# Attention probabilities scaled in place by VectorE before a plain transpose, instead of turned by a matmul with a diagonal

## The reference, cut to what matters

```python
q = apply_rope(split_heads(x @ Wq)); k = apply_rope(split_heads(x @ Wk)); v = split_heads(x @ Wv)
sim = jnp.einsum('bid,bjd->bij', q, k) * scale
sim = jnp.where(causal[None], sim, -jnp.inf)
attn = jax.nn.softmax(sim, axis=-1)
out = jnp.einsum('bij,bjd->bid', attn, v)
```

## Time and profile before

| | us |
|---|---|
| median of three runs | 1790.22 |
| the profiled execution | 1788.28 |
| its span in the trace | 1786.5 |
| PE busy (share) | 1525.2 (85%) |
| DVE busy | 1250.3 (70%) |
| ACT busy | 995.8 (56%) |
| POOL busy | 1019.2 (57%) |

### The profile page before, as it was taken

The page is one execution under the profiler, slowest core; times in us unless marked ns, Lnnn a source line. Parts: engine busy times, 40 slices in busy tenths (PEclk is TensorE's granted clock), DMA queues, the critical chain, the costliest instruction groups (busy, mean ns, idle before and its releaser), DMA issues. The chain is left out here.

```text
span 1786.5 us, 31373 instructions
## 1 busy us (share of the span) xinstructions
PE 1525.2 (85%) x11301; PEld 1440.1 (81%) x11301; DVE 1250.3 (70%) x2526; ACT 995.8 (56%) x2138; POOL 1019.2 (57%) x814
## 2 busy tenths in 40 slices
PE   5389999999999999999499999999998937689129
PEld 4279999999999998998399999999987836688029
DVE  6547676868677877776346766666678569559896
ACT  4547575657575757665355555455544434459552
POOL 4479586969687777864466767766765633000000
PEclk8679999999999999999699999999999968899569
DMA  6490000000001001000465555555554331003313
GB/s 237 147 300 19 18 19 25 31 25 30 25 14 38 13 22 33 4 31 10 154 177 143 144 136 146 135 147 140 140 136 107 71 96 35 18 1 130 104 52 113
DMA packets 86129, 150.44 MB, mean 84 GB/s; under 512 B 7992, under 2 KB 63608, under 8 KB 85720
## 3 DMA queue, kind: packets, MB, share of 16 engines
q1 hardware_dynamic: 75464, 134.62, 24.6%
q0 software_dynamic: 10512, 13.83, 4.6%
HBM read 111.88 MB, written 49.91 MB: 91 GB/s over the span
## 5 line engine op out<-in xcount | busy, mean ns | idle before, releaser
L1534 POOL TENSOR_TENSOR expert_w_low<-expert_raw,expert_w_high 128x768 fp32r<-128x768 f32 x152 | 288.3, 1946 | 170.3 <-ACT expert_w_high L1359 164.3
L835 ACT ACTIVATE expert_raw<-psum,neg_max 120x376 f32<-120x376 f32 (+2 forms) x384 | 176.0, 479 | 99.3 <-DVE neg_max L996 99.2
L664 PE MATMUL psum<-diag,expert_raw 128*128 128x128 f32 (+2 forms) x1536 | 198.9, 279 | 8.2 <-DVE diag L1005 7.3
L1012 DVE TENSOR_TENSOR pt_low<-psum,pt_high 128x752 fp32r<-128x752 f32 x128 | 120.5, 941 | 118.1 <-ACT pt_high L844 118.1
L1506 DVE TENSOR_TENSOR expert_act_low<-expert_act,expert_act_high 128x384 fp32r<-128x384 f32 x152 | 140.1, 921 | 80.0 <-ACT expert_act_high L1397 79.4
L664 PEld LDWEIGHTS psum<-diag,expert_raw 128*128 128x128 f32 (+2 forms) x1536 | 180.3, 190 | 17.9 <-DVE diag L1005 11.2
L1397 ACT ACTIVATE expert_act_high<-expert_act 128x384 fp32r<-128x384 f32 x152 | 79.8, 525 | 204.7 <-DVE expert_act L1501 203.5
L1318 PE MATMUL psum<-slots_high,expert_w_high 128*128 128x384 f32 x608 | 160.1, 344 | 16.6 <-DVE expert_act L1501 15.4
L936 POOL TENSOR_TENSOR qk_low<-rotated,qk_high 128x376 fp32r<-128x376 f32 x128 | 144.1, 1126 | 47.1 <-ACT qk_high L828 44.3
L959 POOL TENSOR_TENSOR rotated<-expert_raw 128x376 f32<-128x376 f32 x128 | 127.9, 1000 | 56.8 <-ACT expert_raw L822 42.6
L1318 PE MATMUL psum<-slots_low,expert_w_high 128*128 128x384 f32 x608 | 156.4, 338 | 0.0
(11 more groups left out here) (296 smaller groups left out, 4422.6 us busy)
## 6 DMA issues: line engine op xcount, KB each, us to landing
expert_raw<-in_experts SPq DMA_DIRECT2D x152, 384.0 KB, 3.1
x_slots<-in_c_slots SPq DMA_DIRECT2D x4, 3168.0 KB, 29.4
slot_rows<-x_slots SPq DMA_DIRECT2D x19, 396.0 KB, 4.6
up_spill<-held SPq DMA_DIRECT2D x5, 1128.0 KB, 5.0
held<-up_spill SPq DMA_DIRECT2D x5, 1128.0 KB, 5.7
attn_x<-tok_xt SPq DMA_DIRECT2D x6, 752.0 KB, 4.0
x_parts<-attn_x SPq DMA_DIRECT2D x6, 752.0 KB, 4.6
patch<-in_patches SPq DMA_DIRECT2D x8, 376.0 KB, 7.0
```

The costliest lines, as they stand in the source:

```text
L664: last = pe.matmul(psum[0:nj, BANK_PT + bank, at:at + ni], probs[0:ni, h % 2, src:src + nj], diag[0:ni, h % 2, it, 0:ni], start=True, stop ...
L835: last = act.activation(probs[0:ni, h % 2, at:at + P * it + ni], score_bank(h % 2, it), ACT.Exp, bias=neg_max[0:ni, h % 2, it:it + 1], acc ...
L1012: dve.tensor_tensor(pt[1][:, h % 2, :, :], psum[:, BANK_PT:BANK_PT + 2, 0:TOK], pt[0][:, h % 2, :, :].bitcast(F32), ALU.subtract).then_inc ...
L1534: pool.tensor_tensor(w[1][:, g % RING, :], raw[:, g % RAW, :], w[0][:, g % RING, :].bitcast(F32), ALU.subtract).then_inc(w_low, 1)
```

## The change

The diagonals go. In their place DVE multiplies each tile of `probs` by the reciprocals of its rows, in place, with a per-row scalar: three `tensor_scalar` operations per head, of 128x128, 128x256 and 120x376. PE's six matmuls per head with the diagonal become six transposes against the constant identity. PE's `turn` waits for the third of the three operations. The `diag` tile (128 x 768 f32) is no longer allocated.

```diff
-        diag = sb("diag", [P, 2, TILES, P])
...
-                    pe.wait_ge(diag_made, 16 * b + h + 1)
+                    pe.wait_ge(probs_scaled, TILES * (16 * b + h + 1))
...
-                            last = pe.matmul(psum[0:nj, BANK_PT + bank, at:at + ni],
-                                             probs[0:ni, h % 2, src:src + nj],
-                                             diag[0:ni, h % 2, it, 0:ni], start=True, stop=True)
+                            last = pe.transpose(psum[0:nj, BANK_PT + bank, at:at + ni],
+                                                probs[0:ni, h % 2, src:src + nj], ident[0:ni, 0:ni])
...
-                def diagonals(b, h):
+                def scale_probs(b, h):
 
                     dve.wait_ge(exp_made, 16 * b + h + 1 + CR_EXP)
                     dve.reciprocal(inv_sum[:, h % 2, 0:TILES], row_sum[:, h % 2, 0:TILES]).then_inc(inv_made, 1)
                     dve.wait_ge(inv_made, 16 * b + h + 1)
-                    dve.tensor_tensor(diag[:, h % 2, :, :],
-                                      ident[:].rearrange("p (o n) -> p o n", o=1).broadcast_to((P, TILES, P)),
-                                      inv_sum[:, h % 2, 0:TILES].rearrange("p (t o) -> p t o", o=1)
-                                      .broadcast_to((P, TILES, P)), ALU.mult).then_inc(diag_made, 1)
+                    for it in range(TILES):
+                        ni, at = TILE_ROWS[it], PROBS_AT[it]
+                        rows_of = probs[0:ni, h % 2, at:at + P * it + ni]
+                        dve.tensor_scalar(rows_of, rows_of, inv_sum[0:ni, h % 2, it:it + 1], None,
+                                          ALU.mult).then_inc(probs_scaled, 1)
```

More of the change, by code:

```diff
@@ L497, in attention @@
          raw_made, swap_made, rope_made, rot_made, qk_high, qk_ready, scores_made, max_made, exp_made,
-         inv_made, diag_made, turned, pt_high, pt_ready, mixed, o_high, o_ready, out_made, out_kept) = (
+         inv_made, probs_scaled, turned, pt_high, pt_ready, mixed, o_high, o_ready, out_made, out_kept) = (
             sem(n) for n in
@@ L501, in attention @@
             "raw_made swap_made rope_made rot_made qk_high qk_ready scores_made max_made exp_made "
-            "inv_made diag_made turned pt_high pt_ready mixed o_high o_ready out_made out_kept".split())
+            "inv_made probs_scaled turned pt_high pt_ready mixed o_high o_ready out_made out_kept".split())
         CR_RAW, CR_ROT, CR_SCORES, CR_EXP, CR_TURN, CR_PT, CR_MIX, CR_O, CR_QK = 1, 2, 4, 1, 2, 1, 2, 1, 2
@@ L1170, in step @@
                     if more or c + 1 < PAIRS:
-                        diagonals(b, 2 * c + 2)
-                        diagonals(b, 2 * c + 3)
+                        scale_probs(b, 2 * c + 2)
+                        scale_probs(b, 2 * c + 3)
                     if projects:
@@ L1183, in _ @@
                 maxima(0, 0)
-                diagonals(0, 0)
-                diagonals(0, 1)
+                scale_probs(0, 0)
+                scale_probs(0, 1)
                 for b in range(BATCH):
```

## The result

The changed kernel takes 1812.76 us (median of four runs, 1812.33 to 1818.67) against 1789.43 us before (four runs). The ratio is 1.0138, 95% interval 1.0116 to 1.016: slower by 1.4%, some 23 us. The execution with the profile is the longest of the four, 1818.67 us with a span of 1816.9; attention, from the first reciprocal of the softmax to that of the last pair of heads, grew in it by 26 us (111.8 to 859.7 us against 111.8 to 833.5), so a few of its 30 us lie elsewhere.

A forecast was written before the change was run, and what follows sets the result against it. POOL was taken to set the plain step at about 9.0 us as much as PE; +48 for 53 blocked stretches and -4 at the end gave +44 on 1788.3, so 1834 us by the runs' median; range 1775 to 1895.

The forecast's parts named there:

- the blocked stretch: Plain attention step, first scaling to end of DVE's swap, scalings waiting behind POOL operations: grows from 2.5 to 4.8 us.
- The walk: Trace of DVE and POOL through one plain attention step: it goes from 9.0 to 9.9 us.
- The second half of the step: Behind the swap in a plain step: POOL's five operations take 5.1 us; DVE needs 4.7 and waits for POOL.
- +0.9 per contended plain step: Scaling stretches in attention that meet a working POOL, 53 counted with scatter steps: +0.9 us each, +48 us in all.
- The scatter steps: Steps of later batches where POOL also has a scatter, 9.9 us before: +0.9 us each, bounds 0 and +1.6.
- The end of attention: Last three steps, without POOL and set by PE: 3 x -1.25, so -4 us.
- POOL sets the pace: Plain attention step: POOL's 8.2 us plus blocking by DVE lets the step fall only from 9.0 to some 8.7 us.
- PE decides: Rival, chance 0.12: scalings in attention find gaps or keep the way open; faster by about 17 us, 1773 us.
- Every scaling loses a whole operation: Rival, chance 0.10: each scaling in attention waits for a whole POOL operation; step 12.3 us, +175 us, 1965 us.
- The loss of clock: Rival, chance 0.05: PE's clock falls to 0.50 in half of the attention steps; +160 us, about 1950 us.

The follow-up runs named there:

- The kernel with the lighter POOL: Changed kernel with POOL's low part of queries and keys made on 128 of 376 columns only, the rest left zero; 1755.11 us, ratio 0.9812.

## Why the prediction was right or wrong

**The sign was right, and so was the mechanism of the blocked stretch.** The forecast said slower because a scaling can stand behind a POOL operation and the stretch then holds back the swap. The walk gave 4.8 us from the first scaling to the swap's end; it is 167.25 - 162.78 = 4.47. It gave the three scalings of the first head until 1.65; they end at 1.62. The step came out at 9.62 instead of 9.9. One detail was other: the fifth scaling slips in before POOL's L957, and the sixth alone waits for it.

**The second half of the step was right in part by luck.** The forecast gave 5.1 us of POOL's five operations behind the swap, with DVE done after 4.7 and waiting for POOL; 172.40 - 167.25 = 5.15. But the scaling at 172.40 waits for nothing: it takes 288 ns. DVE's own way there is 5.15 us, with 0.56 us for ACT's copy in it, a wait that the walk had taken off. The kernel with the lighter POOL says the same: POOL has less to do behind the swap, and what the step loses is just what the scalings lose.

**Shown by runs:** the loss is the sharing (1746.70 us with more work but nothing shared; 58 us won back by a shorter POOL operation against 8), and it is not the transposes (they gain 23 us by themselves). The scalings by themselves cost 38 us with PE's matmuls as before, by 1826.53 against 1788.80 of the kernel before in the same rounds. That it grows with the number of operations (one 1761.90, three 1812.76, four 1834.85) fits, but is not shown by itself: one operation is less bare work as well, and four come with a loss of clock.

**The size was off, 44 us against 23.** The mis-sized terms:
- The +0.9 per contended plain step measured +0.63: 0.3 us too long a stretch.
- The scatter steps were given the same +0.9. In a full batch the seven steps between its reciprocals went from 66.8 to 69.9 us, +3.0 together, not +6.3: the first fell by 0.2, the next three rose by 1.3, 0.7 and 0.6, the fifth fell by 0.7 (PE's routing step, which the transposes shorten), and the last two rose by 0.6.
- The end of attention was credited with -4 us. The last batch grew instead by 4.9 us (777.2 to 833.5 against 798.5 to 859.7), of which its last two steps have +2.5. I took the last three to be PE's. In the first of the two (839 to 851 us) POOL still works and the scalings take 2.16 and 2.13 us, where the diagonals took 1.71 and 1.13; it has +1.8. In the other PE has half its clock until 855.4 us; it has +0.7.

**The step that failed is in the reading of the bound:** "POOL sets the pace at about 9.0 us as much as PE does", and from it that the step could only go to some 8.7 us. POOL's gaps of 0.15 us looked like a full engine. With nothing blocked the step is still 9.00 us with PE's matmuls, and POOL is busy 7.84 of it: PE alone was the bound. With transposes and nothing blocked the step is 8.17 us, and POOL looks as full as before, 7.73 us of it; with 1.1 us less for POOL the step is 8.18. The forecast survived since the change's own step is set by the blocked stretch.

**The rivals.** "PE decides" did not come; the transposes alone would have been near it (1766 against its 1773). "Every scaling loses a whole operation" did not come: in a plain step three of six wait. The loss of clock came only at the end: 1.00 from 145 to 840 us of the changed kernel, with 12 of 72 PE records of a step transposes, then 0.50 from 848.6 to 855.4. That stretch lies in steps that are 2.5 us longer together. What the Trainium skill says of transposes (TensorE: Matmul & The Clock Gate, Part 4), that they do not count as busy time in the same way, can't be told from the effect of idle time here: the kernel with scalings alone, whose PE has no transposes in attention's softmax, is at 0.50 from 856.5 to 859.9 us as well. The Trainium skill's rule on the shared port (SBUF — State Buffer, Who interferes with whom) is borne out by the 403 and 1139 ns of the same 120x376 operation in one step. The same section of the Trainium skill says that an instruction with one SBUF input outside the two-port modes does not contend; the scalings with a PSUM factor bear it out, 384 of 384, and so do the swaps of the changed kernel, 561 to 590 ns in all 128.

## What to carry to other kernels

Before an operation on VectorE is split or moved, look whether GpSimd is busy on the same stretch and whether the new form is one of those that waited here: a `tensor_scalar` from SBUF to SBUF, or two inputs in SBUF. Each such operation can wait for a whole GpSimd operation, but not each does, so walk the order of both engines. A small operand that can live in a free column of PSUM turns it into a form that never waited here, though it is slower when nothing is in the way. And an engine without gaps is a candidate for the bound and no more: only a kernel in which it has less to do shows it. Look at the clock of every stretch that grew, the short ones too.

## What the runs showed of the hardware that was not expected

- Of three scalings in a row with no wait between, not each loses its turn: in the plain step the first, third and fifth run at 0.29, 0.40 and 0.34 us, and the second, fourth and sixth take 1.09, 0.89 and 1.14 us.
- One operation of 120x760 in place took 615 ns at best, 2455 at worst and 1.11 us on average (142.1 us for 128); the same columns in three took 247.4 / 128 = 1.93 us a head.
- With the factor in a PSUM column, 128, 256 and 376 columns took 288, 414 and 539 ns on average, about 1 ns for each added column, against 0.29, 0.34 and 0.40 us at best for the `tensor_scalar` in SBUF.
- Six transposes take 165.09 - 164.46 = 0.63 us to the next projection, less than half of the 1.30 us of the twelve matmul records, with loads of 142 ns on average instead of 190.
- The granted clock fell to 0.50 for short stretches of 3.4 to 10.2 us: in the changed kernel behind 2.46 us of idle PE, and near the same place in a kernel without these transposes too (3.4 us, scalings alone).
